# A gated attention block on one core: moved folds, a reordered prologue and subtractions in the last step

## What is computed

```python
xn = layernorm(x)
Q, K, V = xn @ Wq, xn @ Wk, xn @ Wv              # 16 heads of 64
A = softmax(Q @ K.T / sqrt(64), axis=keys) @ V
s = xn + gelu(A) @ Wpost
g = silu(mx_quantize(xn) @ mx_quantize(weight).T + bias)   # FP6 grid, blocks of 32
out = x + s * g
```

## Time and profile before

| | |
|---|---|
| median of 3 runs | 1375.05 us (1374.01 to 1375.67) |
| profiled execution, its own time | 1378.43 us |
| span of the profiled execution | 1376.6 us |
| PE busy | 1349.0 us, 98% |
| POOL busy | 1176.9 us, 85% |
| DVE busy | 1107.5 us, 80% |
| ACT busy | 759.8 us, 55% |
| chain that ended last | PE 92%, DMA 3%, DVE 2%, ACT 1% |

### The profile page before, as it was taken

The page is one execution under the profiler, slowest core; times in us unless marked ns, Lnnn a source line. Parts: engine busy times, 40 slices in busy tenths (PEclk is TensorE's granted clock), DMA queues, the critical chain, the costliest instruction groups (busy, mean ns, idle before and its releaser), DMA issues.

```text
span 1376.6 us, 26547 instructions
## 1 busy us (share of the span) xinstructions
PE 1349.0 (98%) x10076; PEld 788.5 (57%) x10076; DVE 1107.5 (80%) x1505; ACT 759.8 (55%) x1068; POOL 1176.9 (85%) x551
## 2 busy tenths in 40 slices
PE   7899999999999999999999999999999999999998
PEld 4555555555555555555555555555555555555497
DVE  6688888888888888888888888888888888888523
ACT  4445665555556566555556565555555655555573
POOL 3589999998999989998999989999899999999930
PEclk8999999999999999999999999999999999999999
DMA  2012112211212122211212121211211111211474
GB/s 82 16 42 64 46 61 72 64 43 57 64 42 65 57 62 59 62 59 46 59 57 64 42 65 57 61 45 57 64 42 57 49 48 27 65 49 47 139 251 140
DMA packets 110490, 87.64 MB, mean 64 GB/s; under 512 B 70430, under 2 KB 84510, under 8 KB 110364
## 3 DMA queue, kind: packets, MB, share of 16 engines
q1 hardware_dynamic: 110364, 85.96, 21.2%
HBM read 69.66 MB, written 16.25 MB: 62 GB/s over the span
## 4 chain that ended last, share of the span: by engine, by line
PE 92%; DMA 3%; DVE 2%; issue 1%; ACT 1%; SPq 1%; POOL 0%; DVEq 0%
PE acc L583 33%; PE scores L525 24%; PE peaks L511 13%; PE extra L434 8%; PE scores L532 6%; PE extra L446 4%; PE scores L653 2%; DMA sum_scratch<-group_sums 1%; DVE half_maxes L1043 1%; PE extra L475 1%; DMA inv_scratch<-sums_flat 1%; PE extra L482 0%; DMA probs<-att_scratch 0%; PE extra L457 0%; DMA sums<-sum_scratch 0%
## 5 line engine op out<-in xcount | busy, mean ns | idle before, releaser
L921 POOL TENSOR_TENSOR prob_sum<-prob_sum,probs 128x1024 f32<-128x1024 f32 x384 | 916.9, 2388 | 85.3 <-ACT probs L773 39.9
L1043 DVE TENSOR_REDUCE half_maxes<-peaks 128x2 f32<-128x1024 f32 x504 | 616.5, 1223 | 179.4 <-PE peaks L511 170.1
L773 ACT ACTIVATE probs<-scores 128x1024 f32<-128x1024 f32 x357 | 358.6, 1024 | 501.3 <-PE scores L532 501.3
L583 PE MATMUL acc<-probs,vals 128*64 128x512 f32 x2048 | 492.5, 601 | 0.0
L511 PE MATMUL peaks<-k_hi,q_hi 64*128 64x512 f32 x1008 | 282.7, 457 | 7.3 <-DVE half_maxes L1043 7.1
L525 PE MATMUL scores<-q_hi,k_hi 64*128 64x512 f32 x1024 | 255.1, 397 | 0.0
L525 PE MATMUL scores<-q_lo,k_hi 64*128 64x512 f32 x1024 | 250.4, 391 | 0.0
L525 PE MATMUL scores<-q_hi,k_lo 64*128 64x512 f32 x1024 | 250.4, 391 | 0.0
L583 PEld LDWEIGHTS acc<-probs,vals 128*64 128x64 f32 x2048 | 127.8, 136 | 210.6 <-issue 201.2
L511 PEld LDWEIGHTS peaks<-k_hi,q_hi 64*128 64x128 f32 x1008 | 116.9, 184 | 197.6 <-DVE half_maxes L1043 119.1
L1074 DVE TENSOR_TENSOR probs<-scores,max_rep 128x1024 f32<-128x1024 f32 x155 | 188.2, 1214 | 2.9 <-PE scores L525 2.9
(11 more groups left out here) (166 smaller groups left out, 1219.5 us busy)
## 6 DMA issues: line engine op xcount, KB each, us to landing
max_rep<-max_scratch SPq DMA_DIRECT2D x62, 512.0 KB, 4.0
inv_sum<-inv_scratch SPq DMA_DIRECT2D x128, 128.0 KB, 2.9
att_scratch<-att SPq DMA_DIRECT2D x48, 256.0 KB, 2.3
probs<-att_scratch SPq DMA_DIRECT2D x8, 512.0 KB, 6.2
max_scratch<-turned SPq DMA_DIRECT2D x252, 1.0 KB
split_back<-att_scratch SPq DMA_DIRECT2D x6, 512.0 KB, 5.1
sums<-sum_scratch SPq DMA_DIRECT2D x128, 8.0 KB, 2.2
out_dram<-xn SPq DMA_DIRECT2D x8, 256.0 KB, 4.7
```

Of the source, the lines that this page charges most:

```text
L583: last = mm(acc[own[h], :], vals[(s // 2) % 2][:, j, own[h]], probs[j][:, h, :], start=(k == 0), stop=(k == KT - 1), tile_position=col[h])
L773: sa.activation(probs[j][:, :, :], src[:, :, :], ACT.Exp, scale=DH ** -0.5).then_inc(probs_ready, 1)
L921: gp.tensor_tensor(prob_sum[s % 2][:, :, :], before[:, :, :], probs[order(s)[j]][:, :, :], ALU.add).then_inc(probs_summed, 1)
L1043: v.tensor_reduce(half_maxes[:, :, f // 2, f % 2], peaks[:, :, :], AX.X, ALU.max).then_inc(peaks_read, 1)
```

## The change

It has five parts.

1. The fold of odd steps moves ahead of the reduction of the second peak tile in round 3, in all odd steps but the last. The fold of even steps stays.
2. In the quantisation of a tile one of its steps moves from part 2 to part 1.
3. Prologue: DVE takes all eight first reductions in a row and joins the maxima; the low parts of the second half (`("q", 0, 1)`, `("k", 0, 1)`) come behind, one before and one after the spreading of the first rows. The maxima are turned in `acc` instead of `extra`. PE issues two products of constants into `acc` behind each of four value tiles (`warm`). Score 0 waits for the first two low parts alone.
4. Step 0: each round's second peak tile stands between the two scores, and its third in the middle of the second score; none is left behind the weighing.
5. `by_vector` takes in the last step: tiles 0, 2, 4 and 6 of step 63 are subtracted on DVE.

```diff
-    FILLS = [("v", 0, 0), ("v", 0, 1), ("turn", 0)]
+    FILLS = [("v", 0, 0), ("v", 0, 1)]
...
     def by_vector(s, j):
-        return 0 < s < NS - 1 and j in BY_VECTOR[s % 2]
+        return s > 0 and j in BY_VECTOR[s % 2 if s < NS - 1 else 0]
...
                  ("x", 0, 1): scores[0][:, 1, :], ("q", 0, 1): scores[1][:, 0, :], ("k", 0, 1): scores[1][:, 1, :],
+                 ("turn", 0): acc[:, :]}
...
                 if s == 0 and j == 0:
-                    is_read(pe, ("turn", 0))
+                    pe.wait_ge(rows_spread, 1)
...
-                if j == 0 and s < 2:
-                    pe.wait_ge(lows_ready, 4)
-                elif j == 0:
+                if s == 0 and j < 2:
+                    pe.wait_ge(lows_ready, 2 + 2 * j)
+                elif j == 0 and s > 1:
                     is_read(pe, ("kq"[s % 2], s // 2, 1))
...
+            def warm():
+                for _ in range(2):
+                    mm(acc[:, :], ones_r[:, :], max_rows[0][:, :], start=True, stop=True)
...
             for i in range(3, 7):
                 first_peak(i)
                 project_v(("v", 0, 0), range(i - 3, i - 2))
-            project_v(("v", 0, 1), range(0, 1))
+                warm()
             first_peak(7)
-            project_v(("v", 0, 1), range(1, QT))
+            project_v(("v", 0, 1))
             turn(("turn", 0))
...
                     score(s, 2 * r)
-                    score(s, 2 * r + 1, among(s, r), todo[1] if among(s, r) else None)
+                    if s == 0:
+                        peak(*todo[1])
+                    score(s, 2 * r + 1, among(s, r), todo[2 if s == 0 else 1] if among(s, r) else None)
...
-                    for at in todo[2:3]:
-                        peak(*at)
                     for use in behind:
                         run(use)
-                    for at in todo[3:]:
-                        peak(*at)
...
                     step(v.tensor_tensor(q, q, f, ALU.subtract))
+                    step(v.tensor_tensor(q, q, h, ALU.add))
                 elif part == 2:
-                    step(v.tensor_tensor(q, q, h, ALU.add))
...
-                                extra[:, 0:P].unsqueeze(1).broadcast_to([P, QT, P]),
-                                neg_eye[:, :].unsqueeze(2).broadcast_to([P, QT, P]), ALU.mult).then_inc(extra_read, 1)
+                                acc[:, 0:P].unsqueeze(1).broadcast_to([P, QT, P]),
+                                neg_eye[:, :].unsqueeze(2).broadcast_to([P, QT, P]), ALU.mult).then_inc(rows_spread, 1)
...
-            for i in range(4):
-                first_reduce(i)
-            low(("q", 0, 1))
-            low(("k", 0, 1))
-            for i in range(4, 8):
+            for i in range(8):
                 first_reduce(i)
             join_maxima(0)
+            low(("q", 0, 1))
             dve.wait_ge(consts_loaded, 32)
             spread_first_rows()
+            low(("k", 0, 1))
...
+                    if half == 1 and r == 3 and s < NS - 1:
+                        fold_sums(s - 1)
                     for at in todo[1:2]:
                         reduce_peaks(*at)
...
-                    if r == FOLD_AT[half] and half == 1 and s < NS - 1 and not turns_x:
-                        fold_sums(s - 1)
+                    for at in todo[2:]:
+                        reduce_peaks(*at)
...
-                    if not (half == 1 and s < NS - 1 and not turns_x) and r == (FOLD_AT[half] if s < NS - 1 else 1) and s > 0:
+                    if s > 0 and half == 0 and r == 3 or s == NS - 1 and r == 1:
                         fold_sums(s - 1)
```

More of the change, by code:

```diff
@@ L203, in gated_attention_kernel @@
         consts_set = sem("consts_set")
[L204 removed]
+        first_filled, rows_spread = sem("first_filled"), sem("rows_spread")
         extra_filled, extra_read = sem("extra_filled"), sem("extra_read")
@@ L990, in quantise @@
                 word = lambda a: a.bitcast(mybir.dt.int32)
-                done = [before + (0, 3, 5, 8)[part] + (part > 0 and src is not None)]
+                done = [before + (0, 3, 6, 8)[part] + (part > 0 and src is not None)]
                 def step(ins):
@@ L1149, in _ @@
                         invert_sums(s - 2)
-                    for at in todo[2:]:
-                        reduce_peaks(*at)
                     if half == 0 and r == 0 and n % HP == HP - 1 and later < B:
```

4 lines of the change are left out of this document (1 added, 3 removed).

## The result

| | before | after |
|---|---|---|
| median of the runs | 1374.92 us | 1356.76 us (1354.76 to 1358.11) |
| profiled execution, its span | 1378.43 us, 1376.6 | 1358.11 us, 1356.3 |
| first weighing, step 1's first weighing (starts) | 41.79, 62.32 | 38.69, 57.75 |
| last weighing of step 62 (start) | 1289.68 | 1270.18 |
| mean granted clock | 0.993 | 0.997 |

A forecast was written before the change was run, and what follows sets the result against it. PE, busy 98% of the span, was taken as the bound, so only its waits and slow clock could yield time. -15.1 - 6.0 + 0.8 = -20.3 us, 1358.1 profiled; 3.4 lower for the median: 1354.8 us, range 1350.5 to 1362.5.

The forecast's parts named there:

- -15.1 forecast: Round 0 of even steps: moving the fold removes a surplus of 0.56 us in 27 steps, 15.1 us in all.
- two halves: Round 0's surplus of 0.54 to 0.58 us: projection waits for `extra`, middle peak product for its reduction; both held by DVE.
- rival A: Round 0 of even steps: only `extra` comes free earlier, middle peak product still waits; 7.6 instead of 15.1, 1362.3 us; 12%.
- -6.0 forecast: Prologue and step 0: three terms summing to 6.6 us gained, taken as 6.0 since the clock may fall; bounds 3 and 7.5.
- The turn was put at 25.1: Prologue: the turn of the maxima into rows starts at 25.1 instead of 27.51, 2.4 us gained.
- 12.1 forecast: Prologue, turn to first weighing: 12.1 us at full clock instead of 14.35, with three waits for reductions; 2.3 us gained.
- 1.9 in all: Step 0, first weighing to step 1's: reductions run beside a score, saving 0.6 to 0.7 us in each of three rounds.
- +0.8 forecast: Last step: DVE queues delay the inverse sums, PE's saving is worth nothing; 0.8 us slower, bounds 0 and 2.8.
- B: Prologue gives almost nothing: clock stays at 0.50 through step 0, constant products delay reductions; -1 instead of -6, 1359.8 us; 13%.
- C: The end gives more back: broadcast and later inverse both count and push all later loads; +5, 1359.0 us; 10%.
- D: Low queries not ahead of the fold, or tied to something else; only prologue and end count, 1369.9 us; 4%.
- E: Slower than before: the moved fold outgrows its gap, waiting for a POOL addition and stalling PE in 30 steps; 1421 us; 2%.

The follow-up runs named there:

- lowq_first: The changed kernel with the fold of odd steps put behind the low queries instead of ahead of them: 1379.17 us, ratio to before 1.0035.
- last_only: The kernel before with only the last step's change (its tiles subtracted on VectorE): 1372.79 us, ratio 0.9992 (0.9979 to 1.0005).
- fold_only: The kernel before with only the fold of odd steps moved ahead: 1359.95 us, ratio 0.9883.
- no_warm: The changed kernel without the eight products of constants in the prologue: 1354.09 us, ratio to before 0.9855.
- after_again: The changed kernel itself, run a second time beside later experiments: 1356.22 us, ratio to before 0.9866.
- warm1: The changed kernel with four of the eight products of constants, one behind each value tile instead of two: 1354.71 us, ratio to before 0.9854.

## Why the prediction was right, and where it was not

**The fold in odd steps: right in size, wrong in structure.** -15.1 forecast, -14.9 in the trace, -14.8 alone. It was priced by the whole surplus of the round, and that was sound. The statement that the surplus "has two halves", one for the projection waiting for `extra` and one for the middle peak product, failed: lowq_first gives the first half and gets nothing. The bound of 7.6 and rival A rested on adding two waits of which one lay inside the other.

**The step of the quantisation: zero forecast**, some 0.3 us measured in three rounds. A miss too small to matter.

**The prologue: right in sign, 1.4 too high, and for partly wrong reasons.** -6.0 forecast, -4.6 in the trace. Its three terms:
- The turn was put at 25.1 and came at 26.17. The mis-sized term is the pair of constant products, 0.67 us and not 0.45 (an estimate for which the forecast names no row), a round of 1.47 and not 1.25. Without them the turn is at 24.71.
- From the turn to the first weighing 12.52 us against 12.1 forecast (14.35 before). What I had thought the products would secure, the clock, needed no securing; and the allowance for a later fall of the clock was used: 0.3 us of 0.6.
- "1.9 in all" for the three rounds to step 1 is the step that failed. The rounds did get 1.5 us shorter, but the same reordering costs 1.6 us before the first weighing. I had read a distance between two marks without asking whether the first mark moves. The reading itself was also too even: in the kernel before, the waits behind the three weighings are 1.32, 1.42 and 0.30 us (ahead of the products at 45.48, 52.45 and 59.36), not 1.3 each.

How much of the rest is the clock shows in last_only and fold_only, whose prologue is that of before. In last_only's profile the clock was at 0.50 in 25 to 30 us, as in the earlier trace rows, but back at 0.87 in the next stretch and 1.00 in the one behind it, and its way to step 1 took 33.27 us instead of 35.66. In fold_only's it stayed low for as long as before (0.65 and 0.70 in these two stretches), and the way took 35.62. So 2.4 us of the 3.9 by which the profiled pair differs there depend on how long the clock stays low, and that varies from one execution of the old prologue to the next. That the forecast came within 1.4 us of the pair is in part luck.

**The last step: +0.8 forecast**, -0.8 in the profiled pair, undecided in the runs. The queue on VectorE behind the fold that waits for POOL was foreseen and is there. Its price is the distance between the weighings in rounds 2 and 3 of step 63: 7.54 and 7.14 us in the two profiles of the changed kernel, 4.80 to 4.93 in six others, 4.19 before. Of the 2.7 us by which 7.54 stands above no_warm's 4.85, 1.6 are waiting and 1.1 the fall of the clock behind it. In 13 of the 14 profiles the last stretch of products waits for a transfer of attention tiles, so the price need not reach the end. In the fourteenth, after_again, it did. Its chain of waits:

```profile
1284.37 1.19 DVE probs L1077
...
1288.70 2.46 PE acc L584 x8
...
1293.10 55.92 PE scores L657 x1024
```

Here all 1024 products of the projection run without a gap behind the last weighing, and the chain comes from the subtraction behind the late fold. That the end is paced by transfers alone was the forecast's step, and it does not hold in every execution; how much earlier this end would have come without the wait is not shown.

**The step from the profiled execution to the median** is where the remaining 2 us come from. The sum -20.3 met the profiled pair exactly, by errors that cancel. I then took the 3.4 us by which the old profiled execution stood above its median as a constant. It was not: the new profiled execution stood 1.4 us above its median. Of the 3.4 us, 1.75 are one fall of the clock in the last stretch of products, which 12 of the 13 other profiles do not have; the rest is not traced to a place. In the 44 runs of the kernel before that stand beside the experiments the time goes with the mean granted clock: 1378.3 us on average at 0.992, 1375.4 at 0.995 and 1370.8 at 0.998. The profiled execution had 0.993.

Of the signs that the prediction named, round 0 came at 4.86 us, two steps took 39.1 (1011.22 to 1050.29 in the chain), and the granted clock was 1.00 around 25 us. The turn near 25 and the first weighing near 37 us did not come (26.17 and 38.69).

Rivals: B came nearest among those rejected (the prologue alone is -4.7, not -1). C did not occur: counted from the same product, the last stretch started 0.4 us later behind step 62 than before, and not 5. D is ruled out by the order of VectorE's rows. E is ruled out by the fold's mean of 1235 ns beside GpSimd at work (1236 before); the longest of the 64 took 1245 ns. The rule of the Trainium skill, "SBUF — State Buffer", section "SBUF: two separate sides", of an exclusive lock of the port pair that VectorE and GpSimd share would, if the fold counted among the operations it names, have made some of the 64 wait for a whole addition (2389 ns); the trace gives no sign that it does. The fold reads one tensor of SBUF (`prob_sum`), so by its inputs the rule does not name it.

## What to carry to other kernels

When an instruction waits for two things, do not add the two waits: an edit that removes the earlier one alone gives nothing (lowq_first), and one that removes the later one can give at most what lies between the two, unless it moves the earlier one too, as this change does. When one part of a prologue shortens the distance between two marks, check that it did not push the first mark. And before filling idle time to hold a clock, first remove what makes the idle time: here moving two low parts did it, and the filler cost 1.5 us.

## What the hardware showed that I had not expected

- Two products of constants of 128 rows take 0.67 us from start to next start at full clock, where a pair of products of 64 rows ("x2") is followed by the next pair after 0.24 us. In warm1 one such product takes 0.43 us (19.23 to 19.66), so the second one adds 0.24, as much as a pair of 64 rows.
- The same code has more than one clock history. Of the eleven profiles with the new prologue, four show the clock falling between 30 and 40 us (0.66 to 0.92 in a stretch) and seven do not, at the same waits of 1.35 us; a fall cost 0.3 to 0.9 us. In the last stretch of products two profiles of 14 have one, for 1.4 to 1.8 us, and both profiles of the changed kernel have one in step 63, behind TensorE's wait of 2.3 us. The transfers at the end add their own: in 13 profiles the last stretch of products starts 55.1 to 59.3 us behind step 62's last weighing.
- A late arrival of 128 KB of inverse sums at POOL (2.4 us of waiting instead of 0.8) travels through three engines: POOL's sums, VectorE's fold and the subtraction queued behind it, and a 2.4 us wait of TensorE with a fall of its clock behind. It came in both profiles of the changed kernel and in none of the six others with this last step; why is open.
